# Opening of a transformer layer: products of ones on TensorE during the first loads, small loads issued by ScalarE, first rows in two transfers

## Time and profile before

| what | value |
| --- | --- |
| median of three runs | 939.93 us |
| profiled execution | 940.82 us, of which the span from first to last instruction is 939.1 us |
| busy: PE, PEld, DVE, ACT, POOL | 96%, 84%, 65%, 55%, 36% of the span |
| chain that ended last | PE 82%, DVE 6%, issue 2%, ACT 1%, DMA 1% |
| mean granted TensorE clock | 0.993 |

### The profile page before, as it was taken

How to read it: one execution, slowest core, us unless ns; L and a number is a source line. 1 busy time by engine, 2 the same in 40 slices (tenths; PEclk the granted TensorE clock), 3 DMA queues, 4 the chain that set the end, 5 groups by cost and what they waited for, 6 DMA issues and landing times.

```text
span 939.1 us, 20266 instructions
## 1 busy us (share of the span) xinstructions
PE 899.5 (96%) x6934; PEld 791.3 (84%) x6943; DVE 612.1 (65%) x1457; ACT 518.5 (55%) x1049; POOL 338.5 (36%) x318
## 2 busy tenths in 40 slices
PE   6989998999998999999999899999999999999996
PEld 4678986566555878888989899999999999999996
DVE  4888787898877866666545656565565656565452
ACT  3684424556545555546444666575666657575552
POOL 3467322211302464554553224233242423332222
PEclk9999999999999999999999999999999999999998
DMA  8300020000002121111227255225252522522222
GB/s 243 120 1 1 1 70 21 1 1 1 2 8 91 37 76 59 65 60 59 82 94 250 75 136 135 46 46 135 46 135 46 135 46 46 135 46 46 46 46 34
DMA packets 48943, 63.99 MB, mean 68 GB/s; under 512 B 9985, under 2 KB 41921, under 8 KB 48769
## 3 DMA queue, kind: packets, MB, share of 16 engines
q0 software_dynamic: 17504, 34.87, 15.9%
q1 hardware_dynamic: 31248, 27.46, 9.9%
q10 hardware_dynamic: 144, 1.05, 0.4%
HBM read 38.59 MB, written 24.77 MB: 67 GB/s over the span
## 4 chain that ended last, share of the span: by engine, by line
PE 82%; DVE 6%; issue 2%; ACT 1%; DMA 1%; SPq 0%; POOL 0%; DVEq 0%; POOLq 0%; ACTq 0%
PE PS L136 24%; PE PS L137 23%; PE PS L138 23%; PE PS L873 3%; PE PS L1808 2%; PE PS L917 2%; PE PS L903 1%; PE PS L923 1%; DVE mxpad L1114 1%; DVE hidl L142 1%; DMA xr<-routed_rows 1%; ACT prT L996 1%; DVE oTl L142 1%; PE PS L1343 1%; PE PS L845 0%
## 5 line engine op out<-in xcount | busy, mean ns | idle before, releaser
L1854 ACT ACTIVATE hideh<-PS,be 128x256 fp32r<-128x256 f32 x280 | 140.5, 502 | 153.3 <-PE PS L138 143.8
L1882 POOL DMA_INDIRECT out_rows<-y,toki x70 | 122.9, 1756 | 269.7 <-DVE y L1922 261.2
L142 DVE TENSOR_TENSOR hidel<-act32e,hideh 128x256 fp32r<-128x256 f32 x280 | 118.6, 426 | 107.1 <-ACT act32e L1856 94.3
L136 PE MATMUL PS<-xTeh,wfch 128*128 128x256 f32 x560 | 159.4, 285 | 1.5 <-issue 1.1
L136 PE MATMUL PS<-wprh,hideh 128*128 128x256 f32 x560 | 158.6, 283 | 0.0
L137 PE MATMUL PS<-xTel,wfch 128*128 128x256 f32 x560 | 158.4, 283 | 0.0
L138 PE MATMUL PS<-xTeh,wfcl 128*128 128x256 f32 x560 | 158.4, 283 | 0.0
L137 PE MATMUL PS<-wprl,hideh 128*128 128x256 f32 x560 | 155.6, 278 | 0.0
L138 PE MATMUL PS<-wprh,hidel 128*128 128x256 f32 x560 | 155.5, 278 | 0.0
L1856 ACT ACTIVATE act32e<-PS,be 128x256 f32<-128x256 f32 x280 | 140.9, 503 | 2.8 <-DVE hidel L142 2.8
L136 PEld LDWEIGHTS PS<-xTeh,wfch 128*128 128x128 f32 x560 | 107.3, 192 | 3.1 <-issue 2.6
(11 more groups left out here) (272 smaller groups left out, 2084.8 us busy)
## 6 DMA issues: line engine op xcount, KB each, us to landing
xr<-routed_rows SPq DMA_DIRECT2D x36, 272.0 KB
fcraw<-in_Wfc POOLq DMA_DIRECT2D x8, 1024.0 KB
prraw<-in_Wproj POOLq DMA_DIRECT2D x8, 1024.0 KB
X<-in_x SPq DMA_DIRECT2D x8, 512.0 KB, 6.5
out_rows<-X SPq DMA_DIRECT2D x8, 512.0 KB, 3.0
routed_rows<-pads SPq DMA_DIRECT2D x8, 272.0 KB
out_rows<-y,toki POOLq DMA_INDIRECT x70
ctx<-in_ctxT SPq DMA_DIRECT2D x4, 256.0 KB, 7.0
```

The lines of the kernel that those rows point to most:

```text
L136: nc.tensor.matmul(out, wh, xh, start=first, stop=False)
L142: return eng.tensor_tensor(out, whole, high.bitcast(F32), ALU.subtract)
L1854: nc.scalar.activation(hid[0][:, j, :], PS[:, j % 4, 0:BLK], ACT.Gelu_apprx_tanh, bias=bias)
L1882: nc.gpsimd.indirect_dma_start(out=out, out_offset=bass.IndirectOffsetOnAxis(ap=toki[:, h:h + 1], axis=0), in_=y[:, h, :], in_offset=None, ...
```

## The change

Four edits, all in the first stage. (1) TensorE gets 12 products of `ones` by `ones` (128x128 by 128 columns, f32) into PSUM bank 5 ahead of its wait for `w_in`; their result is read by nobody. (2) VectorE fills `ones` ahead of `onesrow`. (3) The six `w_in` loads are issued by ScalarE, as the first thing in its program, in the order `alog`, `steps`, `bdt`, `dsk`, `wx`, `wdt`; SP issues `win` and what follows right behind `ident` and `small`. (4) `x` of chunk 0 comes in two transfers of two row tiles, each with a semaphore, and VectorE takes `bn_stats` of the first two tiles when the first has landed. The work for chunk 0 no longer adds to the semaphore `bn_waits`.

```diff
--- before.py
+++ after.py
@@ -222,28 +222,27 @@
              t_ready, t_exp, u_ready, u_ln, rates_ready, prod_ready, powers_ready, cU_ready, raw_psum, ksb_ready,
              kern_psum, s_chain, hn_var, hn_rstd, hT_psum, hT_high, hT_low, z_psum, z_copied, sz_ready, win_split,
              wout_split, g_high, g_low, yD_ready, g_ready, o_psum, x1_ready, k_psum, kT_ready, v_psum, v_ready, vz,
-             k_ready, bv_ready, bo_psum, bo_ready) = phase_sems(ctx, """consts_in w_in win_in kv_in wout_in late_in
+             k_ready, bv_ready, bo_psum, bo_ready, x0_rest) = phase_sems(ctx, """consts_in w_in win_in kv_in wout_in late_in
                 small_mm ones_ready alog_ready alog_exp dlt_ready t_ready t_exp u_ready u_ln rates_ready prod_ready
                 powers_ready cU_ready raw_psum ksb_ready kern_psum s_chain hn_var hn_rstd hT_psum hT_high hT_low
                 z_psum z_copied sz_ready win_split wout_split g_high g_low yD_ready g_ready o_psum x1_ready k_psum
-                kT_ready v_psum v_ready vz k_ready bv_ready bo_psum bo_ready""")
+                kT_ready v_psum v_ready vz k_ready bv_ready bo_psum bo_ready x0_rest""")
             W_IN, KV_IN, LATE_IN = 16 * 6, 16 * 7, 16 * 7
             CHUNKS = [slice(16 * i, 16 * (i + 1)) for i in (0, 2, 1, 3)]
             COPIED = 3
             WHOLE = 2
+            WARM = 12
 
             def first_sync(sp, small_loads, up_load, down_load):
                 def x_load(b):
                     sp.dma_start(X[:, b * TB:(b + 1) * TB, :],
                                  d["x"][b].rearrange("(t p) d -> p t d", p=P)).then_inc(x_in[b], 16)
 
-                x_load(0)
+                for h, sem in enumerate((x_in[0], x0_rest)):
+                    sp.dma_start(X[:, 2 * h:2 * h + 2, :],
+                                 d["x"][0, 2 * h * P:2 * (h + 1) * P].rearrange("(t p) d -> p t d", p=P)).then_inc(sem, 16)
                 for dst, src in ((ident[:], d["ident"]), (small[:], d["small"])):
                     sp.dma_start(dst, src).then_inc(consts_in, 16)
-                for dst, src in ((wx[:], d["W_xT"].rearrange("(k p) r -> p k r", p=P)),
-                                 (wdt[:].rearrange("r e g -> r (e g)"), d["W_dtT"]), (bdt[:], d["b_dt"]),
-                                 (dsk[:], d["D_skip"]), (alog[:], d["A_log"]), (steps[:], d["steps"])):
-                    sp.dma_start(dst, src).then_inc(w_in, 16)
                 sp.dma_start(win[:], d["W_inT"].rearrange("(k p) e -> p k e", p=P)).then_inc(win_in, 16)
                 for b in range(1, 3):
                     x_load(b)
@@ -369,8 +368,10 @@
                         if t % 2:
                             last.then_inc(o_psum, 1)
 
+                pe.wait_ge(ones_ready, 1)
+                for _ in range(WARM):
+                    nc.tensor.matmul(PS[:, 5, 0:P], ones[:], ones[:], start=True, stop=True)
                 pe.wait_ge(w_in, W_IN)
-                pe.wait_ge(ones_ready, 1)
                 for k in range(KE):
                     nc.tensor.matmul(PS[0:R, 6, 0:1], wx[:, k, 0:R], ones[:, 0:1],
                                      start=k == 0, stop=k == KE - 1)
@@ -503,9 +504,18 @@
                     dve.wait_ge(g_high, b + 1)
                     low(nc.vector, gl[:, b % SLOTS, :], sz[:, b % SLOTS, :], gh[b % 2][:]).then_inc(g_low, 1)
 
+                nc.vector.memset(ones[:], 1.0).then_inc(ones_ready, 1)
                 nc.vector.memset(onesrow[:], 1.0)
-                nc.vector.memset(ones[:], 1.0).then_inc(ones_ready, 1)
-                stats_part(0)
+                dve.wait_ge(x_in[0], 16)
+                for t in range(2):
+                    nc.vector.bn_stats(stats[:, t, :], X[:, t, :])
+                dve.wait_ge(x0_rest, 16)
+                for t in range(2, TB):
+                    last = nc.vector.bn_stats(stats[:, t, :], X[:, t, :])
+                link(last)
+                for t in range(TB):
+                    last = nc.vector.bn_aggr(mv[:, t, :], stats[:, t, :])
+                last.then_inc(hn_var, 1)
                 dve.wait_ge(w_in, W_IN)
                 nc.vector.tensor_scalar(alog[:], alog[:], 88.7, None, ALU.min).then_inc(alog_ready, 1)
                 apply_part(0)
@@ -657,6 +667,10 @@
                                          PS[:, 6:8, :].rearrange("p c (g a e) -> p a (c g) e", a=NA, e=NE),
                                          ACT.Copy).then_inc(ksb_ready, 1)
 
+                for dst, src in ((alog[:], d["A_log"]), (steps[:], d["steps"]), (bdt[:], d["b_dt"]),
+                                 (dsk[:], d["D_skip"]), (wx[:], d["W_xT"].rearrange("(k p) r -> p k r", p=P)),
+                                 (wdt[:].rearrange("r e g -> r (e g)"), d["W_dtT"])):
+                    nc.scalar.dma_start(dst, src).then_inc(w_in, 16)
                 act.wait_ge(alog_ready, 1)
                 nc.scalar.activation(rate[:], alog[:], ACT.Exp).then_inc(alog_exp, 1)
                 act.wait_ge(win_in, 16)
```

## The result

Slower, not faster. In eight runs each the changed kernel took 944.5 us in the median (941.36 to 945.23) and the kernel before 939.99 (936.79 to 941.79). The ratio is 1.0047, with a 95% interval of 1.0030 to 1.0064, and the time is outside the range forecast. The profiled execution, at 941.36 us with a span of 939.7, is the fastest of the eight, so the traces show the cause of the loss better than its size.

What follows compares the result with a forecast made beforehand. PE, busy 96% of the span, was taken as the bound, its opening held by the `w_in` wait and a low clock. Large products 0.6 us earlier and chunk 1's transposes 1.7 earlier gave 938.2 against 939.93 us, range 934.4 to 941.6.

Steps and rivals of the forecast that it cites:

- Landing of `w_in`: Opening loads: all six `w_in` loads landed by 7.2 us, against 7.37 before, with bounds 5.9 to 11.0.
- Rival C: Opening loads: sharing with `win` and `x` lands `w_in` at 11.0; 2.7 us slower, 942.6 us; chance 0.08.
- The issue order: ScalarE's six loads: issues start at about 0.9 us, the last, `wdt`, issued from 3.8 to 4.35.
- The split: Chunk 0's `x` in two transfers: statistics overlap the second, 0.6 us saved, GpSimd's tile ready at 9.2 instead of 9.84.
- The products of ones: PE's opening: 24 records from about 1.3 us, ending between 6.5 and 7.2, clock up at about 5.8, delaying nothing.
- The clock falls again before the large products: About 5 us of small work and pauses lose the high clock; it rises 3.4 us into the large products.
- the forecast sum: Opening: large products from 13.1 us, chunk 1's transposes at 19.9 against 21.52; 1.7 us saved.
- The saving goes through one to one: From chunk 1's transposes to the end: the whole 1.7 us saving reaches the kernel's time.
- Which costs 1.7 us: Low clock stretches in the opening, near 70 and 524 us: some 3.4 us of dense products each, costing 1.7 us.
- rival B+: As Rival B, and no low clock stretch follows PE's later pause: another 1.7 us, 934.6 us; chance 0.07.
- Rival B: Opening: clock holds through the small work, chunk 1's rows bound its transposes at 17.9; 3.6 us saved, 936.3; chance 0.25.

Runs made afterwards that it cites:

- hold_big: Changed kernel, but SP waits for all six `w_in` loads before issuing `win` and what follows; ratio 0.9999 to the kernel before.
- hold_x: Changed kernel, but SP issues `win`, then waits for all of `w_in` before `x` chunks 1 and 2; ratio 1.0004 to the kernel before.
- loads_only: Kernel before with only the six `w_in` loads moved to ScalarE; ratio 1.0047 to the kernel before.
- split_only: Kernel before with `ones` filled first and `x` of chunk 0 in two transfers, loads on SP; ratio 0.9999 to the kernel before.
- not_moved: Changed kernel with the six `w_in` loads back on SP, products of ones and split kept; ratio 0.9995 to the kernel before.
- ones_only: Kernel before with `ones` filled first and the 12 products of ones, loads and `x` as before; ratio 0.9988 to the kernel before.
- heavy_first: Changed kernel with ScalarE's loads reordered to `wdt`, `wx`, `alog`, `steps`, `bdt`, `dsk`; ratio 1.0037 to the kernel before.
- the held kernels: hold_big and not_moved, each with more products of ones at the start and in PE's pauses; ratios 0.9948 and 0.9963 to the kernel before.
- held_hold: hold_big with 16 products of ones at the start, then 4 and 3 in PE's pauses; 932.57 us against 937.51 for the kernel before, ratio 0.9948.
- held_sp: not_moved with 16 products of ones at the start, then 2 and 3 in PE's later pauses; ratio 0.9963 to the kernel before.

## Why the prediction was wrong, step by step

- **Landing of `w_in`: the step that failed.** "I take 7.2", from `wdt`'s own 3.4 us in the trace of before, where `win` was issued 3 us behind it. The measured value is 11.3, 7.4 us after the issue. This one term, 4.1 us too small, turned the sum from a gain into a loss. The nearest row was not `wdt`'s but `wv`'s, 7.2, issued into full queues as `wdt` now is. I had named the sharing and given it a chance of 0.08, for lack of a count: moving the issues off SP also moves `win` and 1 MB of `x` ahead of the landing of the small loads. hold_big, hold_x and the changed kernel show 2.9, 5.0 and 7.4 us for the same load issued at the same time.
- **Rival C was what happened.** It had 11.0, 17.3 and 24.2 for the landing, the large products and chunk 1's transposes; measured 11.3, 17.63 and 24.79. Its loss of 2.7 was 3.27 in the trace. In the times it is 4.5 with an interval of 2.8 to 6.0, which holds both; loads_only has the same ratio.
- **The issue order**: right to 0.1 us (3.85 for `wdt`).
- **The split**: right in the number, by luck. GpSimd's tile of chunk 0 was ready at 9.3 in the changed kernel (8.08 + 1.23), 9.2 forecast, but it started only 0.28 sooner, not 0.6, and took 1.23 us where 1.48 was reckoned. In split_only it was ready 0.09 sooner, in not_moved 0.64.
- **The products of ones**: right in size, 24 records 0.21 and then 0.11 us apart. They were over at 5.7, sooner than the 6.5 to 7.2 given for the low level, as the clock rose at about 4.5. That moment moves from kernel to kernel: about 4.0 in hold_big, and in not_moved, ones_only and heavy_first all 24 were at the low level and lasted to 6.7 or 6.8.
- **The clock falls again before the large products**: right wherever the 12 products stood alone, at 7.8 in the changed kernel (granted 0.92 in that microsecond and 0.50 in the next, PE idle since 5.7), and at about 9.8, 10.5 and 11.0 in not_moved, ones_only and hold_big, before the large products in each. With the landing at 7.7 the forecast sum came out: chunk 1's transposes at 19.84 in not_moved, 19.9 forecast. That closeness is partly luck: the large products started 0.5 earlier than the 13.1 forecast, and their low records took them 0.45 longer than the 6.8. That this could be mended by a few more products I had not considered.
- **The saving goes through one to one**: right for the loss as far as 320 us; the shift is 3.27 at 24.8 us and 3.23 there. From the pause at 523 on these two traces do not show it; the times do.
- **"Which costs 1.7 us", and rival B+**: wrong for the low stretch at 70. The changed kernel has none behind that pause and gained nothing by it, as VectorE sets the pace there (1.66 behind at 73.4 us, 3.24 again at 78.1). So B+ could not have had its other 1.7 us. The range's lower end is also given as 934.4 for it where its own sum is 934.6.
- **Rival B** was reached by the held kernels alone: 17.9 forecast for chunk 1's transposes with the clock kept, 18.31 and 18.50 measured, and the bound is chunk 1's rows, as it said.

## What to carry to other kernels

When the issue of small loads is moved to a second engine, ask what the first engine will now issue earlier: the loads that everything waits for may then share the DMA engines with the large ones that nobody needs yet. Let the large ones wait for the small ones' semaphore, and read a load's landing from a row with as many bytes in flight. Work that only keeps TensorE's clock up pays when it reaches to the first large product, in every pause on the way; here 12 products at the start were worth 1.0 us, and in hold_big 4 more at the start and 7 in the pauses behind them another 1.9 (20.20 to 18.31).

## What was not expected of the hardware

- A 2 KB load (`dsk`) issued at the end of the queue took 5.7 us to land in heavy_first, against 2.1 to 4.4 us in the other kernels, and `wdt` took 4.9 with a large load right behind it on its own queue.
- In the profiles, low stretches of some 3.4 us appear at other places from kernel to kernel: at 70 and 524 us in the kernel before, at 335.5 (and not at 524) in the changed one, at 67 alone in held_hold, and none between the opening and the end in held_sp. They do not all cost the same: the kernel before loses 1.7 us on the changed one at 524, the changed one 1.4 at 335.5, and the one at 70 is made up for by 78. One profile of each does not tell whether this belongs to the kernel or to the execution. That it is a part of why eight runs of the kernel before lie 5 us apart is argued, not shown, but the times fit: of 32 executions of that kernel on one chip the four fastest (933.82 to 934.57 us) had a mean granted clock of 0.995 to 0.998, the four slowest (939.1 to 941.39) one of 0.992 to 0.994.
